# Splitting the context two steps later, and V projections two steps later, in the cross-attention loop of a Perceiver layer pair

## The reference

```python
Q = _proj(query, Wq, bq)                                # 256 rows, 16 heads of 32
K = _proj(key, Wk, bk)                                  # 25088 rows
V = _proj(value, Wv, bv)
scores = jnp.einsum('bihd,bjhd->bijh', Q, K) * SCALE
attn = jax.nn.softmax(scores, axis=1)                   # over the queries i
x = jnp.einsum('bijh,bjhd->bihd', attn, V).reshape(B, S, D_MODEL)
return x @ Wo + bo
```

## Time and profile before

| what | before |
|---|---|
| time, median of three runs | 2689.59 us |
| time of the profiled execution | 2689.59 us |
| its span, first to last instruction | 2687.9 us |
| PE busy | 2612.9 us (97%) |
| DVE busy | 1967.7 us (73%) |
| ACT busy | 1860.6 us (69%) |
| POOL busy | 1267.2 us (47%) |
| mean granted TensorE clock | 0.991 |

### The profile page before, as it was taken

How to read it: one execution, slowest core, us unless ns; L and a number is a source line. 1 busy time by engine, 2 the same in 40 slices (tenths; PEclk the granted TensorE clock), 3 DMA queues, 4 the chain that set the end, 5 groups by cost and what they waited for, 6 DMA issues and landing times.

```text
span 2687.9 us, 59612 instructions
## 1 busy us (share of the span) xinstructions
PE 2612.9 (97%) x21096; PEld 2204.9 (82%) x21096; DVE 1967.7 (73%) x3889; ACT 1860.6 (69%) x6826; POOL 1267.2 (47%) x2200
## 2 busy tenths in 40 slices
PE   7998999999999999999999999999999998999998
PEld 5775899878888888888888888888888885799997
DVE  6876766577777778777777777777777776655555
ACT  2112444288888888888888888888888886355553
POOL 4432111155556556555655655565555552222222
PEclk9999999999999999999999999999999998999999
DMA  9994445456666666666666666666666653455551
GB/s 340 391 333 184 166 177 191 125 140 172 167 165 157 162 164 161 158 168 166 158 161 165 158 162 168 164 160 162 166 158 161 168 131 125 170 185 188 188 188 71
DMA packets 132300, 473.33 MB, mean 176 GB/s; under 512 B 31129, under 2 KB 31257, under 8 KB 124833
## 3 DMA queue, kind: packets, MB, share of 16 engines
q1 hardware_dynamic: 131616, 468.47, 61.0%
q10 hardware_dynamic: 384, 1.05, 0.2%
HBM read 244.47 MB, written 17.30 MB: 97 GB/s over the span
## 4 chain that ended last, share of the span: by engine, by line
PE 84%; SPq 5%; DVE 3%; DMA 3%; issue 2%; POOL 2%; ACT 1%; ACTq 0%; POOLq 0%; DVEq 0%
PE PB L584 18%; PE PB L609 13%; PE PB L597 11%; PE PB L617 11%; PE PB L685 7%; PE PB L700 6%; PE PB L414 6%; PE PB L546 6%; SPq L332 5%; PE PB L559 3%; DMA STK<-KHL 1%; PE PB L442 1%; PE PB L473 1%; POOL KHL L1484 1%; DMA AR<-in_ctx 1%
## 5 line engine op out<-in xcount | busy, mean ns | idle before, releaser
L825 ACT ACTIVATE EE<-PB,small 128x256 f32<-128x256 f32 x3136 | 1442.6, 481 | 213.6 <-DVE small L1207 199.8
L1207 DVE TENSOR_REDUCE small<-PB 128x2 f32<-128x512 f32 x1568 | 1029.9, 680 | 364.7 <-PE PB L609 364.4
L825 ACT ACTIVATION_READ_ACCUMULATOR EE<-PB,small 128x1 f32 x3136 | 664.3, 212 | 0.0
L1469 POOL TENSOR_TENSOR VS<-V,small 128x128 f32<-128x128 f32 x784 | 319.1, 407 | 710.5 <-DVE small L1213 702.6
L584 PE MATMUL PB<-CTX,WKV 128*128 128x256 f32 x4704 | 625.0, 282 | 3.1 <-POOL CTX L1457 3.1
L584 PEld LDWEIGHTS PB<-CTX,WKV 128*128 128x128 f32 x4704 | 588.4, 190 | 3.4 <-POOL CTX L1457 3.3
L609 PEld LDWEIGHTS PB<-QS,STK 128*128 128x128 f32 x3136 | 469.2, 190 | 127.6 <-issue 60.1
L609 PE MATMUL PB<-QS,STK 128*128 128x256 f32 x3136 | 555.2, 289 | 9.8 <-ACT EE L825 5.0
L597 PE MATMUL PB<-WKV,CTX 128*128 128x512 f32 x1584 | 433.6, 396 | 3.4 <-DVE V L1203 3.4
L617 PE MATMUL PB<-EE,VS 128*32 128x256 f32 x6272 | 382.7, 385 | 0.0
L597 PEld LDWEIGHTS PB<-WKV,CTX 128*128 128x128 f32 x1584 | 273.8, 191 | 40.2 <-DVE V L1203 4.2
(11 more groups left out here) (201 smaller groups left out, 2542.4 us busy)
## 6 DMA issues: line engine op xcount, KB each, us to landing
STK<-KHL SPq DMA_DIRECT2D x1568, 128.0 KB, 2.3
RW<-in_l1f SPq DMA_DIRECT2D x32, 2048.0 KB, 8.1
AR<-in_ctx SPq DMA_DIRECT2D x49, 1024.0 KB, 8.4
RAW<-in_ctx SPq DMA_DIRECT2D x98, 512.0 KB, 3.5
WF<-in_l0f SPq DMA_DIRECT2D x17, 2304.0 KB, 8.8
v_scr<-RAW SPq DMA_DIRECT2D x64, 256.0 KB, 8.2
V<-v_scr SPq DMA_DIRECT2D x64, 256.0 KB, 2.9
WA<-in_l0a SPq DMA_DIRECT2D x1, 4096.0 KB, 12.8
```

Source lines behind the costliest of these rows:

```text
L825: m = e.activation(EE[:, b, s, :], bank(2 * (k % 2) + half, 256 * (s % 2), 256), ACT.Exp, bias=nm[:, b, s:s + 1], accum_out=su[:, b, s:s + 1])
L1207: e.tensor_reduce(nm[:, k % RING, 2 * half:2 * half + 2], bank(2 * (k % 2) + half).rearrange("p (s i) -> p s i", s=2), axis=AX.X, op=ALU.m ...
L1469: e.tensor_tensor(VS[:, b, :].rearrange("p (s d) -> p s d", s=4), V[:, t % 4, 128 * c:128 * c + 128].rearrange("p (s d) -> p s d", s=4), r ...
```

## The change

The V projections move by two steps: each pass of `due_v` comes two steps later, and the one pass that stood ahead of the loop (`project_v(*due_v(-1))`) goes into it. On DVE the two halves of `split_hi` go from steps 2 and 3 to steps 4 and 5. On POOL the four quarters of `split_lo` go from steps 3, 4, 5, 6 to steps 5 (two quarters), 6 and 7. What is computed, and the number of instructions of each kind, stay as they are.

```diff
 def due_v(k):
-    n = (k + 14) // 6
-    return (n, (k + 14) % 6 // 2) if k % 2 and v_tile(n) < NT else None
+    n = (k + 12) // 6
+    return (n, (k + 12) % 6 // 2) if k % 2 and v_tile(n) < NT else None
@@ tensor_program
             for n in range(2):
                 for part in range(3):
                     project_v(n, part)
-            project_v(*due_v(-1))
             w.wait_ge("k_lo", 8)
@@ vector_program
-                if k % 8 in (2, 3) and k // 8 + 3 < NG:
+                if k % 8 in (4, 5) and k // 8 + 3 < NG:
                     split_hi(k // 8 + 3, (k % 2,))
@@ gpsimd_program
-                if 3 <= k % 8 <= 6 and k // 8 + 3 < NG:
-                    split_lo(k // 8 + 3, (k % 8 - 3,))
+                if k % 8 >= 5 and k // 8 + 3 < NG:
+                    split_lo(k // 8 + 3, ((0, 1), (2,), (3,))[k % 8 - 5])
```

## The result

The changed kernel takes 2848.18 us (median of 4 runs, 2846.42 to 2849.28), against 2689.21 us for the kernel before (median of 4, 2682.95 to 2693.04): a ratio of 1.0593, 95% interval 1.0572 to 1.0615. It is slower by 159 us. Forecast were 2829.0 us, in a range from 2783.5 to 2866, and a chance of 0.97 for slower.

A forecast was written before the change was run, and what follows sets the result against it. The PE was taken to bound the loop, busy 1653.86 of 1658.0 us. To 2689.6 us came 143.5 for 95 waits on POOL, less 4.1 of absorbed waits: 2829.0 us, range 2783.5 to 2866.

The forecast's parts named there:

- The walk of POOL's order: Steps 5 to 7 on POOL: released at 1427.28, the last `split_lo` ends at 1432.64, later than the PE wants it.
- POOL's queue as the limit in step 6: Step 6 on POOL: the reciprocal allows 1429.52 without a V output, so POOL's work, not DVE, was taken as limit.
- The size of the term: At step 0's `project_k`: the PE waits 1.51 us for `split_lo`, 95 times, 143.5 us in all.
- The cast ahead of the reciprocal: Step 4 on DVE: `split_hi` ahead of the reciprocal delays POOL's release of step 5 by 0.39 us.
- Absorbed waits for the stacked keys: In the loop: PE waits for late copies, 4.1 us, vanish in front of the longer wait for POOL.
- no waits left on the stacked copies: Sign in the profile after: the PE no longer waits for copies of the stacked keys.
- due_v at nothing: V projections, ahead of the loop and in it: moving them wins or costs 0, at most 1 us.
- Waits of the scores for the exponentials: Step 7 on the PE: perhaps a tenth of a us, only shortening the wait for POOL, so counted 0.
- about 1.5: Sign at `project_k`: about 95 listed PE waits on POOL's `split_lo`, of about 1.5 us each.
- the rival of the falling clock: In the loop: each of 95 waits drops the PE clock, at least 111 us more, 2940 us; chance 4%.
- The other side: In the loop: POOL's new order is fast enough and copies may come earlier, 2685.5 or 2689 us; chance 3%.
- The upper bound: Wait at `project_k` if a cast holds POOL up for its whole length: 1.90 us a block, 180 us.

The follow-up runs named there:

- `k_low` first: The changed kernel with POOL's `k_low` ahead of `scale_v` in step 0: 2846.07 us, ratio 1.0591.

## Why the prediction was right

- *The cause.* The PE waits in step 0 for the last quarter of `split_lo`, once for each of 95 groups, and does not catch up. Shown by the waits at `project_k`, by POOL's part alone (107 us), and by the threshold in the two kernels with more work for POOL.
- *The walk of POOL's order.* Release to end were forecast as 1432.64 - 1427.28 = 5.36 us and are 5.35 in two blocks of three; in the third, with a V output in step 5, they are 1419.42 + 0.73 - 1414.59 = 5.56. This is the step that carried the number.
- *POOL's queue as the limit in step 6.* This reading was wrong for the third block. The prediction let the reciprocal allow 1429.52 "in a block without a V output there" and POOL's work end at 1429.47. But the reciprocal at 1428.49 was read in a block with a V output in step 5, and by the prediction's own numbers it comes 0.05 us behind POOL. So it is in the trace: in such a block `scale_v` of step 6 starts at 1416.98, 0.24 us after the reciprocal at 1416.74, the distance of a `scale_v` that the reciprocal releases (1414.35 to 1414.59, 1433.57 to 1433.81), and 0.12 later than POOL's queue would have let it (the two quarters ahead of it end at 1416.90, and an operation with nothing to wait for starts 0.04 before the end of the one ahead, as at 1436.00). In the block without a V output it is 0.84 after the reciprocal (1435.16 to 1436.00), and there POOL's queue is the limit.
- *The size of the term.* Forecast 1.51 us a block, measured 19.09 - 17.36 = 1.73. This is why the time is 19 us above the number. Three parts were too small. The hand-over from POOL to a waiting PE takes 0.15 us; the 0.06 was read where the PE had waited 3 us. A `project_k` that restarts after the wait takes 1.50 us and not 1.44, and all that releases POOL follows from it: 0.06. And where the cast follows a V output (one block of three), step 5 takes POOL 1416.98 - 1414.59 = 2.39 us and not 1436.00 - 1433.81 = 2.19: the cast meets the two quarters, which last 1.60 us in place of 1.43 (0.17 and not the 0.09 of `scale_v`), and the reciprocal of step 6 holds POOL up for another 0.12. That is 0.20 in one block of three, 0.07 a block. 1.51 + 0.09 + 0.06 + 0.07 = 1.73. All three are small beside the term.
- *The cast ahead of the reciprocal*, 0.39: right, shown in the kernel with both casts behind it.
- *Absorbed waits for the stacked keys.* Forecast 4.1 us, by the period 17.415 - 17.36 = 0.055 a block, 5.2 us. 95 x 1.73 - 5.2 = 159.2, measured 159.0. That these waits cost nothing after the change agrees with `k_low` first, which wins there nothing that can be told. The prediction's sign "no waits left on the stacked copies" did not come true to the letter: between 555 and 2374 us the matmuls still wait for them 4 times, for 1.4 us, where it was 9 times and 3.7 us.
- *due_v at nothing.* Right: putting it back moved 1.9 us, within what runs differ by, and the first `project_k` of the loop still waits 3.5 us without the pass ahead of it.
- *Waits of the scores for the exponentials.* Forecast as a tenth of a us that only shortens the wait behind it. They are 0.23 us a block, twice as much, and they do shorten it: the block's wait on POOL is listed with 1.24 us on average ((120.9 - 3.5) / 95) and not 1.51, while POOL's chain sets the period all the same. Another 0.17 is missing from the listed wait by the modelled end of the scores. The forecast of "about 1.5" for the listed waits missed this, and so did "PE's busy time unchanged": it grew by 46 us, by the same two causes and the slower restart.
- *The rivals.* The loop's granted clock stayed at 1.00 with a wait of up to 1.4 us in every block, so the rival of the falling clock fell. The other side needed POOL to do 5.27 us of work in 3.76; it took 5.35, so that one fell too. The upper bound, in which a cast holds POOL up for its whole length, was 1.90 us a block. The blocks with a V output lose 1.86 (19.22 - 17.36), but 0.15 of that are the hand-over and the restart that the bound left out; the others lose 1.66. The trace bears out that casts and POOL hold each other up, in both directions: the cast at 1415.02, begun while `k_high` ran, took 0.60 us in place of 0.39. It does not show POOL losing the cast's whole length. The rule of the Trainium skill (page SBUF — State Buffer, "SBUF: two separate sides") is that the loser blocks for the other's whole instruction; these rows show less than that.

## What to carry to other kernels

A wait that is not in the profile can still be the next one: put the timelines of the two engines beside each other and read by how much the hand-over is missed, then walk the in-order queue of the producer with its new order from the event that releases it. An engine's mean load says little about it; POOL was busy for under 60% of each block and cost 6%. And a late hand-over in a steady loop is paid once per round where, as here, the producer's release follows from the consumer: such a slip does not heal. Walk it in each kind of block that the loop has, since a release can be the queue's in one and another engine's in the next.

## What the runs showed of the hardware that was not expected

- A PE that waits for POOL's semaphore starts 0.14 to 0.15 us after the record of POOL's instruction ends, in every block read (12 to 13 blocks in each of seven of the kernels, the changed one among them); the 12 matmuls behind it take 0.06 us longer, start to start, than without a wait (1.50 and 1.44).
- POOL and VectorE's cast slow each other by how they are staggered. POOL loses 0.09 us in a `scale_v` that meets one cast (0.49 for 0.40), 0.17 in two `split_lo` that meet the end of one that had itself been held up (1.60 for 1.43; the cast 0.60 for 0.39), and 0.28 in `scale_v` and `k_high` beside two casts (0.49 + 0.59 for 0.40 + 0.40).
